# A four-layer graph network: ScalarE clears two accumulators in pieces, and one small gather moves behind 32 others

## The chip, the cores and the metric

The kernel runs on one core of a Trainium2 chip. The metric is device time in microseconds (us): the median of several runs of the whole kernel. The profile is one further execution, recorded by the hardware profiler. Engines are named PE (TensorE's matmuls), PEld (its weight loads), DVE (VectorE), ACT (ScalarE), POOL (GpSimd) and SP (SyncE). A "q" behind a name (DVEq, SPq) is the engine's sequencer: it fetches instructions, loads register values, waits for semaphores and hands work to the engine.

## The reference, cut to what matters

A graph has 6,250 nodes with 128 features and 206,250 edges, sorted by target node. Four graph layers follow one another, each closed by a residual sum and a layer norm. Every layer sums something over the edges of each node:

```python
# layer 1 (eight heads), per edge: message = src * gate * exp(score)
out1 = segment_sum(message, col); norm1 = segment_sum(exp_scores, col)
# layer 2: out = segment_sum(h[src] * exp(clip(leaky(score)))), and its weights' sum
# layer 3: edge_aggr = zeros.at[row].add(edge_features), then a small MLP per node
# layer 4 (last): per node and head keep the eight best edges, softmax, sum h[col]
out4 = segment_sum(alpha[:, :, None] * x_j, row)
x = layernorm(x + elu(out4))
```

The kernel does the sums of layers 2 and 3 in one pass over the edges.

## The kernel before, in words

Nodes stand in 49 blocks of 128 (`NBX` is 50, with a spare block); edges stand in tiles of 128, and four tiles (`G`) make a group. A segment sum runs over "steps": a step k is a group g of edges together with a node block b, so that a group that crosses a block's edge is seen twice. g and b of each step are read at run time from a small table in SBUF (`step_value`, line 358, a TENSOR_LOAD on the sequencer, and `Blocks`, which holds a block number for later use or loads it again when the ring has come round; with the lag of three steps in layer 1, three of every eight steps load twice).

`stage_aggregate` (layer 1, 451 steps). SP loads a group's 256 KB of messages, POOL multiplies them by their weights (line 1006), DVE builds a one-hot matrix of the edges' nodes (line 1043), ACT puts the weights beside the messages (line 1069), PE multiplies the two into PSUM (line 1083), and DVE adds the result to the accumulator `acc` in SBUF, three steps later (line 1056). Rings are eight deep.

`stage_neighbours` (layers 2 and 3, 464 steps; "layer 2" below). SP loads rows of 520 KB a step into a ring of eight, each load once the matmuls and ACT's copy of the step eight earlier are done. POOL makes the score in five small operations (lines 1656 to 1671, each one step behind the one before it), ACT takes the exponential (`weigh`, line 1682) and keeps two columns (`keep`, line 1689), DVE makes the one-hot matrix (line 1704), the weighted rows (line 1711) and, four steps late, the sum into `acc` (line 1723).

In both stages DVE begins with one memset of the whole accumulator, and the first addition waits for it (`s_z`). `pipeline` writes out such a loop: each part is a function with a lag, and the middle is a hardware loop of eight steps.

`stage_last_layer` starts with three loads on SP's queue (`cur`, `prev`, `nxt`), from which DVE makes flags. Then PE, DVE and ACT look up one score for each edge in 416 groups (the counter `s_look`), DVE ranks the scores, and a loop of 464 steps sums the rows. Beside all that POOL gathers a table row for each edge: 1664 indirect DMAs, four to a group, stored to DRAM by SP and loaded again in the sum's loop. Group g's first gather waits until `s_look` has reached 5g/2. Ahead of the first of them POOL waits for the three loads (`s_fl`) and issues one more indirect DMA, `z_start` (line 1861), whose result is wanted after the last lookup.

Of the kernel before, what the change touches and what calls it, by code (L numbers as in the profile page):

```python
# [20 lines left out]
ACT = mybir.ActivationFunctionType  # L21
# [6 lines left out]
P = 128  # L28
C = 128
# [3 lines left out]
NBX = NB + 1  # L33
NP = NB * P
TE = -(-E // P)
G = 4
# [13 lines left out]
KS = GS + NB - 1  # L50
# [928 lines left out]
        back(1)  # L979


def stage_aggregate(nc, v, name, rows, keys, steps, n_steps, groups, weights, heads, acc):


    R = 8
    s_z, s_ld, s_oh = v.sem(name + "_z"), [v.sem(f"{name}_ld{u}") for u in range(R)], v.sem(name + "_oh")
    s_w, s_wc, s_mm, s_add = v.sem(name + "_w"), v.sem(name + "_wc"), v.sem(name + "_mm"), v.sem(name + "_add")
    s_up = v.sem(name + "_up")
    width = C + heads
    with ExitStack() as mem:  # L990
# [7 lines left out]
        with nc.Block() as block:  # L998
# [31 lines left out]

            @block.vector
            def _(dve):
                nc.vector.memset(acc[:, :, 0:width], 0.0).then_inc(s_z, 1)
                nc.vector.tensor_copy(count_up[:, 0:P], v.iota[:, :]).then_inc(s_up, 1)
                dve.wait_ge(s_up, 1)

                blocks = Blocks(nc, dve, steps, groups, 3, R)

                def prepare(k, u, use):
                    g, b = blocks.load(k, u)  # L1040
                    if later(k, R):
                        dve.wait_ge(s_mm, k - R + 1)
                    nc.vector.scalar_tensor_tensor(  # L1043
                        oh[:, u, :, :], count_up[:, None, 0:P].broadcast_to([P, G, P]), v.blk[:, ds(b, 1)],
                        keys[:, ds(g * G, G), None].broadcast_to([P, G, P]), ALU.add,
                        ALU.is_equal).then_inc(s_oh, 1)

                def add(k, u, use):
                    b = blocks.again(k, u)
                    dve.wait_ge(s_mm, k + 1)  # L1050
                    if later(k, 1):
                        dve.wait_ge(s_add, k)
                    else:
                        dve.wait_ge(s_z, 1)
                    here = flat(acc[:, ds(b, 1), 0:width])
                    nc.vector.tensor_tensor(here, here, ps[u % 4][:, 0:width], ALU.add).then_inc(s_add, 1)

                pipeline(dve, n_steps, (prepare, 0), (add, 3), ring=R)

            @block.scalar  # L1060
            def _(act):
                nc.scalar.preload_act_table(ACT.Copy)

                def put(k, u, use):
                    g = step_value(nc, act, steps, 0, k, groups - 1)
                    if later(k, R):
                        act.wait_ge(s_mm, k - R + 1)
                        act.wait_ge(s_z, 1)
                    nc.scalar.activation(wrow[:, u, :, C:width], weights[:, ds(g * G, G), 0:heads],
                                         ACT.Copy).then_inc(s_wc, 1)  # L1070

                pipeline(act, n_steps, (put, 0), ring=R)

            @block.tensor
            def _(pe):
# [545 lines left out]
def stage_neighbours(nc, v, steps, acc, meta, s_meta):  # L1621


    R = 8
    sem = v.sem
# [4 lines left out]
    with ExitStack() as mem:  # L1630
# [5 lines left out]
        with nc.Block() as block:  # L1636
# [39 lines left out]
            @block.scalar  # L1676
            def _(act):
                nc.scalar.preload_act_table(ACT.Exp)

                def weigh(k, u, use):  # L1680
                    act.wait_ge(s_clip, k + 1)
                    nc.scalar.activation(row[:, u, :, C], t[:, u, 4, :], ACT.Exp).then_inc(s_exp, 1)

                def keep(k, u, use):
                    g = step_value(nc, act, steps, 0, k, GS - 1)
                    act.wait_ge(s_at[u], use * 16 + 16)
                    if later(k, 1):
                        act.wait_ge(s_meta, k)
                    nc.scalar.activation(meta[:, ds(g * G, G), :], row[:, u, :, TAKING:RW], ACT.Copy).then_inc(s_meta, 1)

                pipeline(act, KS, (weigh, 0), (keep, 0), ring=R)

            @block.vector
            def _(dve):
                nc.vector.memset(acc[:, :, :], 0.0).then_inc(s_z, 1)

                blocks = Blocks(nc, dve, steps, GS, 4, R)

                def onehot(k, u, use):
# [15 lines left out]
                def add(k, u, use):  # L1715
                    b = blocks.again(k, u)
                    dve.wait_ge(s_mm, k + 1)
                    if later(k, 1):
                        dve.wait_ge(s_add, k)
                    else:  # L1720
                        dve.wait_ge(s_z, 1)
                    here = flat(acc[:, ds(b, 1), :])
                    nc.vector.tensor_tensor(here, here, ps[u % 4][:, 0:ROW], ALU.add).then_inc(s_add, 1)

# [74 lines left out]
def stage_last_layer(nc, v, gathered, steps, acc):  # L1799
# [4 lines left out]
    sem = v.sem  # L1804
# [17 lines left out]
    with ExitStack() as mem:  # L1822
# [34 lines left out]
        with nc.Block() as block:  # L1857
            @block.gpsimd
            def _(pool):
                pool.wait_ge(s_fl, 48)  # L1860
                nc.gpsimd.indirect_dma_start(
                    out=start[:, :], out_offset=None, in_=v.table[:, :],
                    in_offset=bass.IndirectOffsetOnAxis(ap=cur[:, 0:1], axis=0)).then_inc(s_start, 16)
                for t in range(TS):
                    g, j = t // G, t % G
                    u, use = g % U, g // U
                    if j == 0 and g:

# [767 lines left out]
```

## Time and profile before

| | us |
|---|---|
| median of 3 runs (8676.5 to 8685.21) | 8679.93 |
| the profiled execution | 8693.18 |
| its span in the trace | 8691.1 |
| lies around the span | 2.1 |

| engine | busy us | share of the span |
|---|---|---|
| PE | 5916.9 | 68% |
| PEld | 4854.3 | 56% |
| DVE | 6071.0 | 70% |
| ACT | 1746.5 | 20% |
| POOL | 6425.4 | 74% |

No engine is busy all the time: the stages follow one another, and each has its own limit. A share over the whole span therefore says little about a change in one stage; the windows of a stage, the waits in it and the timeline of its start say more. The time of a sequencer's own instructions is not counted as busy time of its engine. "Idle before ... issue" in a timeline means that the engine waited for nothing that the trace shows as a release, only for its next instruction to come.

### The profile page before, as it was taken

The numbers are of one execution on the slowest core, as the hardware profiler recorded it, in microseconds if no ns is written. First come the engines' busy times: TensorE is split into PE (matmuls) and PEld (weight loads), VectorE is DVE, ScalarE is ACT, GpSimd is POOL, SyncE is SP. The second block draws the span as 40 slices with busy tenths as digits, with TensorE's granted clock in tenths as the row PEclk, the third lists the DMA queues.
The fourth block names the chain that finished last, engine by engine and source line by source line (L and its number), as shares of the span: only waits on it lengthen the run. The fifth ranks groups of instructions, "written<-read, shape, count | busy, mean of one in ns | idle before, by whom it ended". The sixth has DMA issues, their size and how long they took to land. (4 is left out here: it accounts for less than half of the span.)

```text
span 8691.1 us, 192168 instructions
## 1 busy us (share of the span) xinstructions
PE 5916.9 (68%) x40472; PEld 4854.3 (56%) x40473; DVE 6071.0 (70%) x12108; ACT 1746.5 (20%) x5063; POOL 6425.4 (74%) x7809
## 2 busy tenths in 40 slices
PE   6666666665788587777777549999588830566442
PEld 4455555553677466666666437777378720455332
DVE  5555555556777887777777448888599899898335
ACT  1111111111211444444444102222500010111000
POOL 6777777776788377777777778887277778877774
PEclk6555555555899799999999669999799965899555
DMA  6778888875477266666666669998189953798664
GB/s 198 218 216 219 219 217 220 218 219 168 130 210 211 70 212 205 207 206 206 207 206 207 211 196 268 273 270 239 35 245 263 260 145 87 197 255 237 163 163 110
DMA packets 1900193, 1739.84 MB, mean 200 GB/s; under 512 B 163065, under 2 KB 1624495, under 8 KB 1899807
## 3 DMA queue, kind: packets, MB, share of 16 engines
q1 hardware_dynamic: 1216980, 816.75, 32.2%
q10 hardware_dynamic: 496812, 471.17, 19.3%
q0 software_dynamic: 186160, 449.72, 18.5%
q14 instruction: 212, 1.74, 0.1%
q8 instruction: 29, 0.48, 0.0%
HBM read 1285.39 MB, written 452.43 MB: 200 GB/s over the span
## 5 line engine op out<-in xcount | busy, mean ns | idle before, releaser
L1877 POOL DMA_INDIRECT z_xg<-table,srci x1664 | 1781.6, 1071 | 512.7 <-issue 457.4
L1414 POOL DMA_INDIRECT sorted<-e_score,srci x1612 | 1628.2, 1010 | 602.8 <-issue 427.2
L461 POOL DMA_INDIRECT g_xg<-table,srci x1612 | 1553.9, 964 | 539.5 <-issue 470.0
L481 PE MATMUL g_psg<-g_wg,g_eT 128*128 128x136 f32 x3224 | 1027.5, 474 | 0.0
L1957 PE MATMUL z_ps<-z_wrow,z_oh 128*128 128x132 f32 x3712 | 652.1, 330 | 501.9 <-issue 332.6
L1735 PE MATMUL n_ps<-n_row,n_oh 128*128 128x257 f32 x3712 | 881.2, 389 | 93.2 <-DVE n_row L1711 79.3
L1957 PEld LDWEIGHTS z_ps<-z_wrow,z_oh 128*128 128x128 f32 x3712 | 559.4, 228 | 594.6 <-issue 557.3
L481 PEld LDWEIGHTS g_psg<-g_wg,g_eT 128*128 128x128 f32 x3224 | 769.3, 324 | 191.9 <-issue 191.9
L1735 PEld LDWEIGHTS n_ps<-n_row,n_oh 128*128 128x128 f32 x3712 | 677.7, 190 | 298.0 <-issue 216.4
L479 PE MATMUL g_psg<-g_bias,g_ones 3*128 3x272 bf16 x806 | 318.4, 395 | 675.6 <-DVE g_es L570 646.8
L1473 PE MATMUL m_psx<-acc,e_score 128*128 x3608 | 600.5, 317 | 197.8 <-DVE e_score L1598 122.9
L568 DVE TENSOR_TENSOR g_y<-g_psg,g_xg 128x512 f32<-128x512 f32 x403 | 278.5, 691 | 604.7 <-DMA g_xg<-table,srci 590.0
L1473 PEld LDWEIGHTS m_psx<-acc,e_score 128*128 128x128 f32 x3608 | 507.9, 217 | 259.3 <-issue 258.3
L1913 PE MATMUL z_ps<-z_tab,z_ohlo 128*128 128x200 bf16 x4992 | 599.6, 249 | 74.4 <-DVE z_e L2059 69.7
L1598 DVE SCALAR_TENSOR_TENSOR e_score<-e_score,follows,m_psx 128x516 f32 x451 | 339.4, 753 | 370.6 <-ACT e_score L1524 312.2
L522 ACT ACTIVATE g_psg<-g_psg 128x512 f32<-128x512 f32 x403 | 234.5, 582 | 1807.6 <-PE g_psg L481 1807.6
L1083 PE MATMUL ag_ps<-ag_wrow,ag_oh 128*128 128x136 f32 x3608 | 488.9, 289 | 101.2 <-DVE ag_oh L1043 101.1
L2138 DVE TENSOR_TENSOR z_wrow<-z_buf,z_e 128x512 f32<-128x512 f32 x464 | 317.6, 684 | 334.9 <-DMA z_buf<-gathered 334.7
L1463 PE MATMUL m_psl<-m_cnt,e_score 128*128 128x100 f32 x3224 | 550.4, 299 | 0.2 <-DVE e_score L1573 0.2
L1006 POOL TENSOR_TENSOR ag_wrow<-ag_buf,e_score 128x512 f32<-128x512 f32 x451 | 467.6, 1060 | 99.7 <-PE ag_ps L1083 88.5
L479 PEld LDWEIGHTS g_psg<-g_bias,g_ones 3*128 3x128 bf16 x806 | 79.3, 98 | 800.0 <-issue 764.9
L1083 PEld LDWEIGHTS ag_ps<-ag_wrow,ag_oh 128*128 128x128 f32 x3608 | 444.4, 190 | 145.8 <-issue 114.3
(426 smaller groups left out, 12696.0 us busy)
## 6 DMA issues: line engine op xcount, KB each, us to landing
n_row<-sorted SPq DMA_DIRECT2D x464, 520.0 KB, 4.4
z_buf<-gathered ACTq DMA_DIRECT2D x464, 256.0 KB
g_keys<-dst_row ACTq DMA_DIRECT2D x451, 256.0 KB, 3.8
ag_buf<-gated SPq DMA_DIRECT2D x451, 256.0 KB, 3.3
m_keys<-dst_row ACTq DMA_DIRECT2D x451, 256.0 KB
gathered<-z_xg SPq DMA_DIRECT2D x416, 256.0 KB
gated<-g_y SPq DMA_DIRECT2D x403, 256.0 KB
g_eT<-in_attr_t SPq DMA_DIRECT2D x402, 256.0 KB
```

Source lines behind the costliest of these rows:

```text
L461: nc.gpsimd.indirect_dma_start(out=xg[:, u, j, :], out_offset=None, in_=v.table[:, :], in_offset=bass.IndirectOffsetOnAxis(ap=v.srci[:, t: ...
L479: nc.tensor.matmul(psg[u % 2][:, h, 0:H * W], ones[:, :], bias[:, :], start=True, stop=False)
L481: last = nc.tensor.matmul(psg[u % 2][:, h, j * W:(j + 1) * W], eT[:, u % R, (h * H + j) * P:(h * H + j + 1) * P], wg[:, :], start=False, s ...
L1006: engine.tensor_tensor(wrow[:, u, :, 0:C].rearrange("p t (h c) -> p t h c", h=heads), buf[:, u, :, :].rearrange("p t (h c) -> p t h c", h= ...
L1083: last = nc.tensor.matmul(ps[u % 4][:, 0:width], oh[:, u, j, :], wrow[:, u, j, 0:width], start=(j == 0), stop=(j == G - 1))
L1414: nc.gpsimd.indirect_dma_start(out=v.sorted[:, :], out_offset=bass.IndirectOffsetOnAxis(ap=place[:, t:t + 1], axis=0), in_=rows[:, u, j, : ...
L1463: nc.tensor.matmul(to, oht[:, u, j * P:(j + 1) * P], before, start=True, stop=False)
L1473: last = nc.tensor.matmul(psx[u % 2][:, j // 2, (j % 2) * WH:(j % 2 + 1) * WH], hot_t[:, u, j * P:(j + 1) * P], flat(held[:, ds(b, 1), :]) ...
L1735: last = nc.tensor.matmul(ps[u % 4][:, 0:ROW], oh[:, u, j, :], row[:, u, j, 0:ROW], start=(j == 0), stop=(j == G - 1))
L1877: nc.gpsimd.indirect_dma_start(out=xg[:, u, j, :], out_offset=None, in_=v.table[:, :], in_offset=bass.IndirectOffsetOnAxis(ap=v.dsti[:, t: ...
L1913: nc.tensor.matmul(to, ohlo[:, u, edges], tab[:, n, :, :], start=(n == 0), stop=False)
L1957: last = nc.tensor.matmul(bank[u % 4 // 2][:, u % 2, 0:width], oh[:, u, j, :], wrow[:, u, j, 0:width], start=(j == 0), stop=(j == G - 1))
```

## The change

In the two stages the memset on DVE goes. ACT writes the zeros instead, as four copies of a constant zero, each over a quarter of the accumulator's blocks (12, 13, 12 and 13). In layer 1 a piece follows each of ACT's first four steps. In layer 2 the first piece comes ahead of the loop, and the other three follow the first three steps. The addition of a step waits for as many pieces as its block can lie in (1 to 4), and this wait stands in every addition, also in the hardware loop, where it is for 4; before, only the first addition waited for `s_z`. ACT's own wait for `s_z` in layer 1 goes. In the last layer, the wait for the three loads and the `z_start` gather move from POOL's start to the front of group 8, behind 32 gathers.

```diff
+def zero_pieces(nc, v, acc, width, sem):
+
+
+    def zero(n, u, use):
+        a, z = (NBX * n // 4, NBX * (n + 1) // 4)
+        nc.scalar.activation(acc[:, a:z, 0:width], v.zeros[:, None, 0:1].broadcast_to([P, z - a, width]),
+                             ACT.Copy).then_inc(sem, 1)
+
+    return zero
+
+
+def zeroed(k):
+
+    return 4 if not isinstance(k, int) else min(4, sum(k >= NBX * n // 4 for n in range(4)))
...
 def stage_aggregate(nc, v, name, rows, keys, steps, n_steps, groups, weights, heads, acc):
-                nc.vector.memset(acc[:, :, 0:width], 0.0).then_inc(s_z, 1)
...
                     if later(k, 1):
                         dve.wait_ge(s_add, k)
-                    else:
-                        dve.wait_ge(s_z, 1)
+                    dve.wait_ge(s_z, zeroed(k))
...
                     if later(k, R):
                         act.wait_ge(s_mm, k - R + 1)
-                        act.wait_ge(s_z, 1)
...
-                pipeline(act, n_steps, (put, 0), ring=R)
+                pipeline(act, n_steps, (put, 0), (zero_pieces(nc, v, acc, width, s_z), 0, 4), ring=R)
...
 (stage_neighbours)
-                pipeline(act, KS, (weigh, 0), (keep, 0), ring=R)
+                zero = zero_pieces(nc, v, acc, 2 * C + 1, s_z)
+                zero(0, 0, 0)
+                pipeline(act, KS, (weigh, 0), (keep, 0), (lambda n, u, use: zero(n + 1, u, use), 0, 3), ring=R)
...
-                nc.vector.memset(acc[:, :, :], 0.0).then_inc(s_z, 1)
...
                     if later(k, 1):
                         dve.wait_ge(s_add, k)
-                    else:
-                        dve.wait_ge(s_z, 1)
+                    dve.wait_ge(s_z, zeroed(k))
...
 (stage_last_layer)
-                pool.wait_ge(s_fl, 48)
-                nc.gpsimd.indirect_dma_start(
-                    out=start[:, :], out_offset=None, in_=v.table[:, :],
-                    in_offset=bass.IndirectOffsetOnAxis(ap=cur[:, 0:1], axis=0)).then_inc(s_start, 16)
                 for t in range(TS):
                     g, j = t // G, t % G
+                    if t == 8 * G:
+                        pool.wait_ge(s_fl, 48)
+                        nc.gpsimd.indirect_dma_start(
+                            out=start[:, :], out_offset=None, in_=v.table[:, :],
+                            in_offset=bass.IndirectOffsetOnAxis(ap=cur[:, 0:1], axis=0)).then_inc(s_start, 16)
```

## Rows read from the trace of the kernel before

**Rows 1.** Windows of two stretches: from:to us, then the columns of the first line.
```profile
core 0: us, PE busy (x) PEld busy (x) DVE busy (x) ACT busy (x) POOL busy (x), PEclk, DMA share, GB/s
2247.00:2860.00 613.00, 507.65 (x3761) 462.42 (x3760) 453.04 (x913) 116.91 (x465) 492.24 (x474) 0.97 0.67 197
5145.00:6065.00 920.00, 881.22 (x3712) 677.66 (x3712) 781.99 (x1391) 193.77 (x928) 767.43 (x2318) 1.00 0.91 264
```

**Rows 2.** Timeline, layer 1's start: start us, us, engine, line, operation, [idle before, releaser].
```profile
2289.45 5.72 DVE L1033 MEMSET acc<- 128x6800 f32 x1 [33.13 <-issue]
2291.66 1.06 POOL L1006 TENSOR_TENSOR ag_wrow<-ag_buf,e_score 128x512 f32<-128x512 f32 x1 [9.64 <-DMA ag_buf<-gated]
2295.86 2.76 DVE L1043 SCALAR_TENSOR_TENSOR ag_oh<-ag_up,blk,keys 128x512 f32<-128x512 f32 x4 [0.49 <-DVE ag_up L1034]
2296.67 12.85 PE L1083 MATMUL ag_ps<-ag_wrow,ag_oh 128*128 128x136 f32 x88 [29.48 <-DVE ag_oh L1043]
```

**Rows 3.** Timeline of VectorE (DVE) in layer 1's loop, one-hot instructions.
```profile
2330.11 0.75 DVE L1043 SCALAR_TENSOR_TENSOR ag_oh<-ag_up,blk,keys 128x512 f32<-128x512 f32 x1 [0.54 <-issue]
...
2331.11 0.75 DVE L1043 SCALAR_TENSOR_TENSOR ag_oh<-ag_up,blk,keys 128x512 f32<-128x512 f32 x1
...
2332.10 0.75 DVE L1043 SCALAR_TENSOR_TENSOR ag_oh<-ag_up,blk,keys 128x512 f32<-128x512 f32 x1
```

**Rows 4.** VectorE's sequencer (DVEq) by line, layer 1: count, ns min/median/max, first and last start.
```profile
L358 DVEq TENSOR_LOAD <-steps_e x632: 296/302/326, 2295.4 to 2857.1; - x158
L358 DVEq FUSED_REGOPS  x540: 57/57/64, 2315.5 to 2850.7; - x180
...
L1052 DVEq EVENT_SEMAPHORE  x396: 21/21/21, 2300.0 to 2857.4; - x198
L1052 DVEq ALU_OP  x54: 40/40/40, 2316.0 to 2843.4; - x54
...
L1056 DVEq FUSED_REGOPS  x451: 57/57/71, 2298.9 to 2857.5; - x151
...
L1043 DVEq FUSED_REGOPS  x469: 46/186/199, 2295.8 to 2855.2; - x157
L1043 DVEq ALU_OP  x432: 40/40/40, 2315.4 to 2851.4; - x144
```

**Rows 5.** The same for a loop of stage_move whose instructions wait for three semaphores.
```profile
L1594 DVEq EVENT_SEMAPHORE  x1: 21/21/21, 3001.7 to 3001.7; - x1
...
L1596 DVEq EVENT_SEMAPHORE  x450: 49/262/5072, 3005.5 to 5080.3; - x150
```

**Rows 6.** Timeline, layer 2's start.
```profile
5132.99 10.77 DVE L1695 MEMSET acc<- 128x12850 f32 x1 [41.60 <-issue]
...
5137.44 6.92 POOL L1656 TENSOR_TENSOR n_t<-n_row 128x4 f32<-128x4 f32 x1 [2.94 <-DMA n_row<-sorted]
...
5146.93 0.21 ACT L1682 ACTIVATE n_row<-n_t 128x4 f32<-128x4 f32 x1 [15.40 <-POOL n_t L1671]
```

**Rows 7.** Windows, layer 2's start.
```profile
5145.00:5148.00 3.00, 0.00 (x0) 0.02 (x1) 0.83 (x2) 0.42 (x2) 3.00 (x15) 0.50 0.04 13
```

**Rows 8.** Waits in layer 2: engine, line, releaser: us in total, times, longest.
```profile
DVE n_oh L1704 <- issue: 38.0, 131, 0.4
```

**Rows 9.** ScalarE's longest plain fp32 pass (last layer's update), by line.
```profile
L1163 ACT ACTIVATE up_T<-up_T x1: 5538/5538/5538, 8621.6 to 8621.6; 128x6400 f32<-128x6400 f32 x1
```

**Rows 10.** Timeline of GpSimd (POOL) at the last layer's start.
```profile
6298.85 2.53 POOL L1861 DMA_INDIRECT z_start<-table,z_cur  x1 [17.99 <-DMA z_nxt<-sorted_row]
...
6319.27 0.94 POOL L1877 DMA_INDIRECT z_xg<-table,srci  x1 [5.94 <-PE z_ps L1914]
```

**Rows 11.** The last layer's 1664 gathers by line, and waits ahead of them.
```profile
L1877 POOL DMA_INDIRECT z_xg<-table,srci x1664: 939/946/14414, 6301.7 to 8594.7; - x185
...
  issue: 457.4, 1501
...
  PE z_ps L1914: 12.9, 24
```

## The prediction

> **What bounds the kernel now.** I read the windows by stage first, then the timeline at each place the diff touches, then the sequencers' rows by line, and last the waits.
>
> In layer 1 no engine fills its window: PE is busy 507.65 of 613.00 us, POOL 492.24, DVE 453.04 [rows 1]. The timeline says what is missing. In DVE's loop a one-hot starts 0.99 us after the one before it, or, in other steps, only after 0.54 us of idle time put down to issue [rows 3]. The sequencer explains both. It makes 632 register loads of 302 ns in 451 steps, that is 451 and 181 second ones, about three in eight steps [rows 4]; the steps with a second load are the slow ones. A short step has one load (302), one FUSED_REGOPS at L358 (57), one at L1056 (57), one at L1043 (186), one ALU_OP (40) and one EVENT_SEMAPHORE (21): 663 ns [rows 4]. The step is 990 ns [rows 3], so 327 ns for six instructions, 54 ns each, pass between them. The EVENT_SEMAPHORE at L1052 is 21 ns at minimum, median and maximum in all 396 cases [rows 4]: it never waits for PE. The reader is to see that **the DVE sequencer, not an engine, sets layer 1's pace**, so that each instruction put into this loop is paid in full.
>
> In layer 2 DMA moves 264 GB/s, with PE busy 881 and DVE 782 of 920 us [rows 1], 1.98 us for each of 464 steps. DVE's idle time for issue is 38.0 us in 131 steps [rows 8]: there the sequencer is late in little more than a quarter of the steps.
>
> In the last layer POOL's gathers run from 6301.7 to 8594.7 [rows 11], and nearly all their idle time is the 0.3 us between two of them (457.4 us, 1501 times). Only one wait is real: the fifth gather waits 5.94 us for the lookups [rows 10]. **POOL's stream sets this layer's end.**
>
> **The change part by part.** The sum is made against the profiled execution (8693.18 us: span 8691.1 and 2.1 around it), which is 13.3 us above the median of 8679.93; the difference is carried over to the median.
>
> *Layer 1, the start.* The memset (5.72 us) goes, and the one-hots can begin near 2290 in place of 2295.86 [rows 2]. What is late next is POOL: its first product ends at 2291.66 + 1.06 = 2292.72. PE can start then in place of 2296.67: **-3.9 us**. ACT pays for the zeros. A long fp32 pass there takes 5538 ns for 6400 elements, 0.87 ns each [rows 9]; a piece has 1632 or 1768, so 1.4 to 1.5 us and some 0.2 to start. Four pieces with ACT's own small copies are done about 8 us after the first copy; PE's fourth step can't come before 2292.7 + 3 x 1.2, when ACT's fourth copy is done. Nothing. If PE had to wait for ACT in each of the four, the start would gain 1 us less or so.
>
> *Layer 1, the loop.* The new wait is one constant comparison in each addition. The trace has no such addition with three waits here, but it has the pattern elsewhere. Where an instruction waits for two semaphores, one EVENT_SEMAPHORE of 21 ns stands ahead of it, the other wait riding on an instruction that is there anyway [rows 4]. Where it waits for three, the row is still one EVENT_SEMAPHORE for each of the 450 steps, of 49 ns at least; the first step, with two waits, has 21 [rows 5]. So the third wait costs 28 ns in seven of eight steps. In the eighth, 54 times, there is no EVENT_SEMAPHORE now, since an ALU_OP at L1052 carries a wait [rows 4]; with three waits one has to be added: 21 + 54 = 75 ns. Sum: 397 x 0.028 + 54 x 0.075 = 11.1 + 4.1 = **+15.2 us**. Bounds: 0, if the wait rides on an instruction that is there; 451 x 0.075 = +33.8 if each gets an instruction of its own. I take the middle, as row 5 is this very pattern on this very engine. ACT's removed wait gives nothing, since ACT waits for PE.
>
> The Trainium skill, "Advanced Engine Details and Errata" (Network/Comms), gives 50 to 100 ns for the sequencer to read a semaphore. By that the 451 waits would cost an estimated 23 to 45 us; rows 4 and 5 show less for an added wait, so it stands beside the first rival below and not in the sum.
>
> *Layer 2, the start.* The memset of 10.77 us ends at 5143.76, and a POOL operation on 128x4 elements, 6.92 us long, lies under it to 5144.36; the first exponential follows at 5146.93 [rows 6]. From 5145 to 5148 the DMA queues are all but idle (0.04): the eight slots are full and the first isn't free [rows 7]. Without the memset the first exponential may come some 5 us earlier. But three of ACT's pieces, 3084 to 3341 elements, 2.9 us each by the same price, stand between its first four steps, each some 1 us over the pace of 1.98: 3 us are lost again, and only then do the earlier loads count. I take **-4 us**; bounds -7 (the whole idle stretch is filled) and +3 (POOL is no earlier and ACT's pieces delay three steps).
>
> The Trainium skill, "SBUF — State Buffer", says that a DVE instruction with at most one SBUF input outside the two-port modes doesn't contend with GpSimd. The 6.92 us of rows 6 speak against it, the 1.06 us of POOL under layer 1's memset in rows 2 for it. By the rule POOL is no earlier, and the upper bound of this term would hold.
>
> *Layer 2, the loop.* The same wait, 464 times. It can be felt where DVE stood idle for issue: 131 x 0.028 = 3.7 us, half of it hidden since DMA, POOL and PE share the limit: **+2 us**. Bounds: 0, and 407 x 0.028 + 57 x 0.075 = +16 if all are felt.
>
> *Last layer.* Before the fifth gather POOL has time to spare; there `z_start` is free now, and its removal gives nothing. Among the 32nd and 33rd it is not: 0.94 + 0.30 us of a stream that never waits, **+1.2 us**. Its wait for the three loads is long over by then, and its row is wanted only after the last lookup. The first four gathers can now issue some 10 us earlier, while the three loads are in flight (POOL stands idle for 17.99 us until they land [rows 10]). Four gathers of 128 x 136 fp32 are 0.28 MB; at the 0.26 MB per us of rows 1 they can hold the last load back by 1.1 us, and with it flags, lookups and the fifth gather. I take **+0.8**, bounds 0 and 1.1.
>
> **Sum:** -3.9 + 15.2 - 4 + 2 + 1.2 + 0.8 = **+11.3 us**, 8704.5 for a profiled execution and **8691 us** for the median, 0.13% up. A measurement of this kernel can tell about 0.2%, that is 17.4 us, from no change.
>
> **The rivals.**
> 1. *Each added wait is an instruction of its own* (75 ns). For it: the eighth steps. Against it: rows 5. Layer 1's loop costs 33.8 in place of 15.2: the sum is +29.9, 8710 us, slower. It decides from about 47 ns per wait: there layer 1's loop costs 21.3 and the sum passes 17.4.
> 2. *The wait is free*: it rides on the FUSED_REGOPS that computes the address of `acc`. For it: the compiler already lets waits ride. Against it: that instruction is there now, and an EVENT_SEMAPHORE stands ahead of it all the same. Only the starts and the last layer are left: -3.9 - 4 + 2 = -5.9, 8674 us, no change that can be told.
> 3. *Layer 2 pays in full*: the sequencer is late there more often than 131 steps show, and POOL gains nothing at the start. +3 and +16 in place of -4 and +2: the sum is +32, or +23 with one half of each, 8703 us, slower. Against it: the sequencer has no load to repeat in five of eight steps, and 264 GB/s of DMA is near another limit.
> 4. *The starts give much more than their idle time*, because a ring that fills earlier runs steadier: faster by 20 us, 8660. Nothing in the rows speaks for it.
>
> **How the numbers follow.** My case 0.60, its own range 8682 to 8700, with an eighth of it past 17.4 us; rival 1 0.17; rival 2 0.12; rival 3 0.07; rival 4 0.04. Slower by over 0.2%: 0.08 + 0.17 + 0.05 = 0.30; faster by over 0.2%: 0.04 and a little of rival 2, 0.05; within 0.2%: 0.65. The range leaves out rival 4 and the far ends of 1 and 3: 8673 to 8713.
>
> **What would show it.** Layer 1's DVEq row of the new wait's line: EVENT_SEMAPHORE in all 450 steps at 49 or 50 ns (my case), twice as many rows of 21 ns (rival 1), or none added (rival 2). PE's first matmul of layer 1 some 3.9 us sooner after ACT's table load, and the stage from there to its end some 15 us longer. Layer 2's first exponential some 5 us sooner after its table load, the next three about 3 us apart, the DMA queues not idle. The fifth gather no earlier than now, the last one later by 1 to 2 us. The prediction is wrong if layer 1's loop isn't bound by the sequencer in the steps where I say so: then PE or POOL swallows the 28 ns, and the gain at the starts is what is left.

## The result, and the profile after

The changed kernel takes **8695.15 us** (median of 20 runs, 8684.74 to 8707.39); the kernel before, run beside it, 8682.02 (20 runs, 8669.02 to 8695.0). The ratio is **1.0015** with a 95% interval of 1.0009 to 1.0022, that is +13.1 us, with +8 to +19 in the interval. The forecast was +11.3 and 8691: slower, by less than 0.2%.

The profiled execution took 8695.34 us, with a span of 8693.6. That is only 2.5 us above the span before (8691.1), and the reader should not take it for the effect: the first instruction of layer 1 (ACT's table load) comes at 2287.97 before and at 2282.91 after, although nothing is changed ahead of it. A single profile has several microseconds of such scatter outside the changed stages, so everything below is measured from a mark inside the stage.

Layer 1's start after, a timeline (the columns are those of rows 2). L987 is the line of the clearing pieces:

```profile
2282.91 1.28 ACT L1076 ACT_TABLE_LOAD   x1 [19.80 <-PEq L650]
...
2283.74 2.76 DVE L1058 SCALAR_TENSOR_TENSOR ag_oh<-ag_up,blk,keys 128x512 f32<-128x512 f32 x4 [0.50 <-DVE ag_up L1049]
...
2284.34 1.54 ACT L987 ACTIVATE acc<-zeros 128x1632 f32<-128x1632 f32 x1
...
2286.50 1.06 POOL L1022 TENSOR_TENSOR ag_wrow<-ag_buf,e_score 128x512 f32<-128x512 f32 x1 [9.55 <-DMA ag_buf<-gated]
...
2287.66 12.64 PE L1096 MATMUL ag_ps<-ag_wrow,ag_oh 128*128 128x136 f32 x81 [25.55 <-POOL ag_wrow L1022]
...
2289.16 1.66 ACT L987 ACTIVATE acc<-zeros 128x1768 f32<-128x1768 f32 x1
2289.97 0.30 DVE L1070 TENSOR_TENSOR acc<-acc,ag_ps 128x136 f32 x1 [3.47 <-PE ag_ps L1096]
```

PE's first matmul waited for DVE's one-hot before [rows 2]; now its releaser is POOL's product, which is what the prediction named as late next. The one-hots follow DVE's small copy at once. The matmul comes 3.45 us after ACT's first copy (2284.20 to 2287.66), where it was 7.40 us before (2289.26 to 2296.67 [rows 2]): 3.95 us sooner.

Layer 1's loop after, by line on VectorE, sequencer and engine: count, ns min/median/max, first and last start. The first row is the line of the new wait.

```profile
L1068 DVEq EVENT_SEMAPHORE  x451: 21/50/50, 2286.1 to 2863.7; - x151
...
L1070 DVEq FUSED_REGOPS  x451: 57/57/71, 2289.9 to 2863.8; - x151
L1070 DVE TENSOR_TENSOR acc<-acc,ag_ps x451: 282/285/298, 2290.0 to 2863.9; 128x136 f32 x151
```

Where 396 events of 21 ns stood [rows 4], 451 stand now, and their median is 50. Counted one by one, 396 of them take 49 or 50 ns and 55 take 21: the first step, and the 54 eighth ones, in which an event has been added. From the first to the last address computation of the additions (FUSED_REGOPS) it is 573.9 us (2289.9 to 2863.8) in place of 558.6 (2298.9 to 2857.5 [rows 4]): 15.3 us longer. The short steps, in a timeline of VectorE:

```profile
2559.31 0.75 DVE L1058 SCALAR_TENSOR_TENSOR ag_oh<-ag_up,blk,keys 128x512 f32<-128x512 f32 x1
2559.98 0.28 DVE L1070 TENSOR_TENSOR acc<-acc,ag_ps 128x136 f32 x1
2560.33 0.75 DVE L1058 SCALAR_TENSOR_TENSOR ag_oh<-ag_up,blk,keys 128x512 f32<-128x512 f32 x1
2561.00 0.29 DVE L1070 TENSOR_TENSOR acc<-acc,ag_ps 128x136 f32 x1
2561.34 0.75 DVE L1058 SCALAR_TENSOR_TENSOR ag_oh<-ag_up,blk,keys 128x512 f32<-128x512 f32 x1
```

A one-hot starts 1.02 and 1.01 us after the one before it, against 1.00 and 0.99 in rows 3. From the additions' starts in the middle 400 steps, a turn of eight takes 10.218 us after and 9.951 before: 0.267 us more, where the terms of the prediction make 7 x 0.028 + 0.075 = 0.271.

Layer 2's start after, a timeline:

```profile
5134.06 1.28 ACT L1691 ACT_TABLE_LOAD   x1 [45.83 <-PEq L2506]
...
5135.35 2.77 ACT L987 ACTIVATE acc<-zeros 128x3084 f32<-128x3084 f32 x1
...
5138.13 0.75 DVE L1717 SCALAR_TENSOR_TENSOR n_oh<-iota,blk,n_row 128x512 f32<-128x512 f32 x1 [42.90 <-DMA n_row<-sorted]
5140.70 0.21 POOL L1669 TENSOR_TENSOR n_t<-n_row 128x4 f32<-128x4 f32 x1 [2.43 <-DMA n_row<-sorted]
...
5144.69 0.21 ACT L1695 ACTIVATE n_row<-n_t 128x4 f32<-128x4 f32 x1 [6.57 <-POOL n_t L1684]
...
5145.25 2.97 ACT L987 ACTIVATE acc<-zeros 128x3341 f32<-128x3341 f32 x1
...
5148.13 0.19 ACT L1695 ACTIVATE n_row<-n_t 128x4 f32<-128x4 f32 x1
...
5150.98 0.19 ACT L1695 ACTIVATE n_row<-n_t 128x4 f32<-128x4 f32 x1
...
5154.06 0.19 ACT L1695 ACTIVATE n_row<-n_t 128x4 f32<-128x4 f32 x1
```

POOL's second operation takes 0.21 us in place of 6.92 [rows 6]. The first exponential comes 10.63 us after ACT's table load (5134.06 to 5144.69), before it was 16.68 (5130.25 to 5146.93 [rows 6]): 6.05 us sooner. DVE's first one-hot comes 4.07 us after the table load; before, it came at the memset's end, 13.43 us after:

```profile
5143.68 1.28 DVE L1704 SCALAR_TENSOR_TENSOR n_oh<-iota,blk,n_row 128x512 f32<-128x512 f32 x2
```

ACT's pieces then space the exponentials 3.44, 2.85 and 3.08 us apart; before, they came 1.9 us apart, so at the fourth one 3.7 of the 6.05 us are given back. They don't stay lost: the next two exponentials follow within 0.6 us, and the tenth one comes 32.10 us after the table load, before 36.08, a lead of 4.0 us.

The DMA queues show what the earlier start is worth. Both kernels first fill the eight free slots, at some 355 GB/s. Then the queues stand idle until a slot comes free: 7.5 us before, 1.5 us after. Windows of these idle stretches (columns as in rows 1), first before, then after, with the end of the filling ahead of each:

```profile
5138.25:5143.25 5.00, 0.00 (x0) 0.00 (x0) 5.00 (x1) 0.00 (x0) 5.00 (x1) 0.50 1.10 356
5145.00:5152.50 7.50, 4.49 (x11) 3.59 (x12) 4.07 (x6) 1.25 (x6) 7.50 (x26) 0.50 0.01 5
...
5143.80:5147.50 3.70, 1.73 (x4) 1.48 (x5) 1.35 (x2) 2.57 (x3) 3.14 (x14) 0.50 1.09 355
5149.00:5150.50 1.50, 1.50 (x7) 1.17 (x6) 0.71 (x2) 1.50 (x1) 1.50 (x7) 0.69 0.02 8
```

The last layer, a timeline of POOL: the fifth large gather, and the small one in its new place:

```profile
6312.18 0.94 POOL L1890 DMA_INDIRECT z_xg<-table,srci  x1 [26.60 <-PE z_ps L1927]
...
6347.07 0.94 POOL L1890 DMA_INDIRECT z_xg<-table,srci  x1 [0.30 <-issue]
6348.32 0.94 POOL L1876 DMA_INDIRECT z_start<-table,z_cur  x1 [0.30 <-issue]
6349.57 1.06 POOL L1890 DMA_INDIRECT z_xg<-table,srci  x1 [0.30 <-PE z_ps L1927]
```

All large gathers by line, the first and last start behind the durations:

```profile
L1890 POOL DMA_INDIRECT z_xg<-table,srci x1664: 940/944/14412, 6280.7 to 8596.9; - x185
```

The first gather starts at 6280.7, 0.6 us after the first of the three loads is issued (6280.06); before, it was 14 us (6287.73 to 6301.7 [rows 11]). The fifth gains nothing from it: it starts 32.12 us after that issue (6312.18), against 31.54 before (6319.27 [rows 10]). `z_start` sits in a stream without slack, 1.25 us of it.

### The profile page after: what moved, and what is told of

It reads as the page before. It is cut to its first block and busy times, and to the rows that moved or that the text cites. A ratio compares the mean times of both kernels' runs of the same rounds, so it can differ in the third digit from the quotient of the medians.

```text
span 8693.6 us, 191841 instructions
## 1 busy us (share of the span) xinstructions
PE 5937.6 (68%) x40472; PEld 4881.8 (56%) x40473; DVE 6053.8 (70%) x12106; ACT 1761.5 (20%) x5071; POOL 6413.4 (74%) x7809
## 3 DMA queue, kind: packets, MB, share of 16 engines
q1 hardware_dynamic: 1216980, 816.75, 31.9%
## 5 line engine op out<-in xcount | busy, mean ns | idle before, releaser
L1476 PE MATMUL m_psl<-m_cnt,e_score 128*128 128x100 f32 x3224 | 559.0, 302 | 0.1
L1476 PEld LDWEIGHTS m_psl<-m_cnt,e_score 128*128 128x128 f32 x3224 | 526.2, 205 | 2.2 <-issue 0.3
```

What stands on the lines that cost most here:

```text
L1476: nc.tensor.matmul(to, oht[:, u, j * P:(j + 1) * P], before, start=True, stop=False)
```

## The experiments

Each kernel was timed against the kernel before in the same session, or has a single profiled run (numbers 1, 8 and 9), whose time alone says little. The table puts the stages of all profiles side by side. Its numbers are differences of two instructions' starts in one trace: (a) layer 1, ACT's first copy to PE's first matmul; (b) layer 1, first to last addition; (c) layer 2, last gather of the stage ahead to the first exponential; (d) the same gather to layer 2's last addition; (e) last layer, issue of `z_cur`'s load to the last addition.

| kernel | a | b | c | d | e |
|---|---|---|---|---|---|
| before | 7.40 | 558.6 | 24.5 | 941.3 | 2320.9 |
| before, again | 7.41 | 558.8 | 24.5 | 940.5 | 2323.5 |
| layer 1: the wait alone | 7.41 | 573.2 | 24.5 | 938.4 | 2319.3 |
| layer 1: two waits | 7.41 | 612.5 | 24.6 | 944.5 | 2311.3 |
| layer 1: pieces, no wait in the loop | 3.64 | 559.2 | 24.5 | 940.7 | 2322.3 |
| layer 2 as changed | 7.41 | 558.3 | 18.5 | 937.3 | 2317.2 |
| layer 2: pieces, no wait in the loop | 7.40 | 558.5 | 18.6 | 933.9 | 2316.9 |
| layer 2: memset in ten | 7.41 | 558.7 | 19.0 | 935.5 | 2311.9 |
| layer 2: one-hots behind the memset | 7.40 | 558.6 | 18.7 | 941.1 | 2322.3 |
| the small gather alone | 7.41 | 558.6 | 24.5 | 941.3 | 2322.8 |
| changed | 3.45 | 573.9 | 18.4 | 929.6 | 2331.0 |
| changed, again | 3.52 | 573.7 | 18.1 | 940.4 | 2326.2 |
| changed, no waits in the loops, early gather | 3.76 | 559.0 | 18.1 | 934.0 | 2324.2 |
| the same, layer 2's pieces ahead | 3.47 | 559.4 | 20.6 | 934.9 | 2320.6 |

Columns a, b and c hardly scatter between kernels that share the edit (by 0.3, 0.7 and 0.5 us at most). Columns d and e scatter by 6 and 12 us where the stage's code is that of before, and that sets what can be said of them. Column d can be divided at the 40th addition of layer 2. From the last gather ahead to that addition it takes 109.5 to 111.4 us in the six profiles with layer 2 as before (mean 110.6), 104.9 to 105.3 in the three with the pieces and the wait, 104.2 to 106.0 in the three with the pieces and no wait in the loop, 106.0 in number 8 and 108.5 in number 9. Nearly all the scatter of column d lies behind that addition.

**1. The kernel before, once more.** No edit: how far does one profile lie from another?

> The kernel before, unchanged, profiled once more: it gives the size of what one stage's length differs by between two executions. If layer 2's loop (20th to 440th addition, 827.5 us in the first profile) and the last layer (from its first load to its last addition, 2320.9 us) come back within 2 us, the 6 us by which layer 2's loop was shorter and the 10 us by which the last layer was longer after the change are the change's; if they differ by 5 to 10 us, they are the spread of single executions. Layer 1's loop (20th to 440th addition, 523.45 us) should come back within 0.3 us on the theory that a sequencer paces it, since nothing there waits for memory.

Measured: 8692.48 us in one run, span 8690.5. Every column but the last agrees within 0.9 us with the first profile. The last layer differs by 2.6 us, layer 2 by 0.9. What follows: layer 1's length is a quantity that can be read to a microsecond. Two profiles are too few for the scatter of the others; the whole table shows more.

**2. Layer 1: the wait alone.** The memset on DVE stays, and the comparison stands in each addition:

```diff
-                    else:
-                        dve.wait_ge(s_z, 1)
+                    dve.wait_ge(s_z, 1)
```

> The kernel before with one edit: in layer 1 every addition also waits for the memset's semaphore, which has long been set. Theory (the DVE sequencer paces the loop and pays 28 ns for a third wait, 75 ns where none had an instruction of its own): layer 1's loop is 15 us longer, its start and all else as before, 8697 us, ratio 1.0017. Rival (the 15 us of the changed kernel come from ACT's pieces or from chance): no change, 1.000.

Measured: 1.0019, interval 1.0010 to 1.0028 (medians 8719.90 and 8706.62). VectorE by line in layer 1:

```profile
L1053 DVEq EVENT_SEMAPHORE  x451: 21/50/50, 2295.9 to 2869.7; - x151
...
L1055 DVE TENSOR_TENSOR acc<-acc,ag_ps x451: 282/286/298, 2296.7 to 2869.9; 128x136 f32 x151
```

The row of the event is the one of the changed kernel, to the nanosecond, and the loop is 573.2 us long: +14.6 over before. Its wait is for a count reached before the first matmul, so nothing is waited for; reading it is the whole cost. What follows: the wait alone makes the slowdown of layer 1.

**3. Layer 1: the pieces without the wait in the loop.** The pieces are done within ten steps, so only the steps written out ahead of the hardware loop need to look:

```diff
-                    else:
-                        dve.wait_ge(s_z, 1)
+                    if isinstance(k, int) and k < 16:
+                        dve.wait_ge(s_z, 4 if k >= 8 else zeroed(k))
```

> Layer 1's accumulator is cleared by ACT in four pieces as in the changed kernel, but only the additions ahead of the hardware loop wait for them (the ninth for all four); layers 2 and last are those before. Theory: the start gains 3.9 us, the loop is as before (523.5 us from the 20th to the 440th addition), so 8678 us, ratio 0.9996. Rival (the pieces on ACT themselves lengthen the loop): 8692 us, 1.001 or more.

Measured: 0.9999, interval 0.9990 to 1.0008. The start is 3.8 us shorter (column a), the loop 0.4 to 0.6 longer (b), and the hardware loop has its events of 21 ns again. Twelve steps written out ahead of it have events of 49 or 50 ns, which is most of these 0.4 to 0.6 us. What follows: start and loop are two separate terms, and the first can be had without the second. The timed ratio alone could not have told -3.3 us from nothing.

**4. Layer 1: two added waits.** Number 2 with a second comparison:

```diff
+                    dve.wait_ge(s_z, 1)
+                    dve.wait_ge(s_up, 1)
```

> The kernel before with two constant waits more in every addition of layer 1, four in all. Theory: the third wait shares the EVENT_SEMAPHORE of the second (28 ns more), the fourth needs another instruction (75 ns more): 0.103 x 451 = 46 us in layer 1's loop, 8728 us, ratio 1.0054. Rival (28 ns for each wait whatever their number): 25 us, 1.0029. Second rival (75 ns each): 68 us, 1.0078.

Measured: 1.0066, interval 1.0051 to 1.0081; layer 1's loop 612.5 us, +53.9. VectorE's events by line:

```profile
L1053 DVEq EVENT_SEMAPHORE  x396: 21/21/21, 2299.9 to 2911.1; - x198
L1054 DVEq EVENT_SEMAPHORE  x451: 49/50/50, 2298.1 to 2911.2; - x151
```

The third wait of an instruction lengthened an event that was there, from 21 to 50 ns; the fourth needs one of its own. And the waits ahead of DVE and POOL, engine, line, releaser: us in total, times, longest:

```profile
POOL ag_wrow L1006 <- PE ag_ps L1083: 125.1, 219, 0.8
...
DVE ag_oh L1043 <- issue: 126.4, 230, 0.7
```

DVE stands idle for its sequencer 230 times, where it is 94.1 us in 176 in the changed kernel, and POOL waits for PE, which waits for DVE. The second wait cost 39.3 us (612.5 - 573.2). Of these 1.6 us are the 55 events that grow from 21 to 50 ns only now; the rest is 95 ns for each of the 396 further events, more than the 75 ns forecast for an event and its gap, and the 53.9 us are 8 more than the 46 expected. By the additions' starts in the middle 400 steps, five of a turn's eight steps are 0.067 to 0.071 us longer than in the changed kernel, about the forecast price; one is no longer, and two are longer by 0.17 and 0.19. What those two wait for is not settled. What follows: a price near rival 1's exists, one wait further on.

**5. Layer 2 as changed, the rest as before.**

```diff
+                zero(0, 0, 0)
+                pipeline(act, KS, (weigh, 0), (keep, 0), (lambda n, u, use: zero(n + 1, u, use), 0, 3), ring=R)
...
-                nc.vector.memset(acc[:, :, :], 0.0).then_inc(s_z, 1)
...
+                    dve.wait_ge(s_z, zeroed(k))
```

> Layer 2 alone as in the changed kernel (ACT clears in pieces, every addition waits for them); layer 1 and the last layer are those before. The profiles of the kernels before and of three others so far have layer 2 at 938.4 to 944.5 us from the last gather of the stage ahead of it to its last addition, the changed kernel 929.6. Theory (the first exponential comes 6 us sooner, and the loop's rest is little changed): 930 to 936 us for that stretch, 8674 us on the scale of the first median, ratio 0.9993. Rival from the prediction (the added wait is felt in the loop): 945 us or more, ratio 1.001.

Measured: 0.9996, interval 0.9987 to 1.0005. The first exponential is 6.0 us sooner (c), layer 2 ends 4.0 us sooner (d), at 937.3 us: just above the 930 to 936 that were expected, well below the rival's 945.

**6. Layer 2: pieces, no wait in the loop.** Number 5, and in its addition:

```diff
-                    dve.wait_ge(s_z, zeroed(k))
+                    if isinstance(k, int) and k < 16:
+                        dve.wait_ge(s_z, 4 if k >= 8 else zeroed(k))
```

> As the run before, but only the additions ahead of layer 2's hardware loop wait for the pieces. Theory (the wait is mostly hidden in this layer): the stretch is 0 to 2 us shorter than with the wait. Rival (each of the 464 waits is paid, 28 or 75 ns): 10 to 16 us shorter.

Measured: 0.9993, interval 0.9984 to 1.0002; column d 933.9. The two differ by 3.4 us in one profile each and by 0.0003 in time, both inside the scatter. Over all profiles with the pieces, the three with the wait in layer 2's loop have a mean of 935.8 us in column d and the three without it 933.9 to 934.9, mean 934.2. What follows: the wait costs 1.5 us in layer 2 by these means, and a term of +2 is neither confirmed nor refuted; the 16 us of rival 3 would show, and don't.

DVE's idle time for issue, which the prediction used for this term [rows 8], can't tell: 38.0 us in 131 steps before, 34.6 in 114 in the changed kernel. In layer 1, where the same wait made the loop 15.3 us longer, that row hardly moved either. The rows of layer 1, before and changed, and of layer 2, changed:

```profile
DVE ag_oh L1043 <- issue: 93.4, 176, 0.6
DVE ag_oh L1058 <- issue: 94.1, 176, 0.6
...
DVE n_oh L1717 <- issue: 34.6, 114, 0.5
```

All 451 steps of layer 1 paid, not the 176 that this view counts as idle for issue.

**7. The small gather alone.** The last layer's edit, nothing else.

```diff
-                pool.wait_ge(s_fl, 48)
-                nc.gpsimd.indirect_dma_start(
...
+                    if t == 8 * G:
+                        pool.wait_ge(s_fl, 48)
+                        nc.gpsimd.indirect_dma_start(
```

> The small gather of the last layer behind eight groups, all else as before. Theory: three loads land about 1.1 us later, the fifth gather starts 0.6 us later counted from the first load, and one gather of 1.25 us more stands in POOL's stream: 1 to 2 us, which a single execution can't show beside the spread of this layer's lookups and gathers (2311 to 2324 us so far); ratio 1.0002. Rival (the last layer's extra 10 us in the changed kernel's profile come from the move): ratio 1.001, the layer at 2330 us again.

Measured: 1.0005, interval 0.9996 to 1.0014. DVE's flags, which need the three loads, start 11.8 us after the first load's issue, against 10.9 before; the stretch from the 5th to the 101st gather takes 124.5 us, against 122.7. The whole layer takes 2322.8 us, inside the scatter of unchanged code and below the rival's 2330. The timed interval holds both the expected 1.0002 and the rival's 1.001.

**8. Layer 2: the memset in ten pieces on DVE.** Does a memset hold POOL, as the prediction read rows 6? Each piece is 1.13 us:

```diff
-                nc.vector.memset(acc[:, :, :], 0.0).then_inc(s_z, 1)
+                for n in range(10):
+                    last = nc.vector.memset(acc[:, 5 * n:5 * n + 5, :], 0.0)
+                last.then_inc(s_z, 1)
```

> The kernel before with layer 2's memset on DVE cut into ten of 1285 elements, 1.1 us each. Theory (the memset holds POOL's operations back while it runs, as a DVE one-hot with two SBUF inputs does): POOL's second operation no longer lasts 6.9 us but ends with the slice it meets, and the first exponential comes 1 to 3 us sooner after ACT's table load (16.7 us before). Rival (what holds POOL is the one-hot behind the memset, or a load that hasn't landed): the second operation still ends only after the last slice, and the first exponential stays at 16.7 us.

Measured: 8682.06 us in one run. Timeline:

```profile
5138.78 1.13 DVE L1696 MEMSET acc<- 128x1285 f32 x1 [0.22 <-issue]
5140.13 1.13 DVE L1696 MEMSET acc<- 128x1285 f32 x1 [0.22 <-issue]
5140.26 0.21 POOL L1656 TENSOR_TENSOR n_t<-n_row 128x4 f32<-128x4 f32 x1 [2.92 <-DMA n_row<-sorted]
5140.43 0.26 POOL L1660 TENSOR_SCALAR n_t<-n_t 128x4 f32<-128x4 f32 x1
...
5145.32 1.92 POOL L1667 TENSOR_TENSOR n_t<-n_t 128x4 f32<-128x4 f32 x1
5145.51 1.13 DVE L1696 MEMSET acc<- 128x1285 f32 x1 [0.22 <-issue]
5146.56 1.29 DVE L1706 SCALAR_TENSOR_TENSOR n_oh<-iota,blk,n_row 128x512 f32<-128x512 f32 x2
```

POOL's operation runs in 0.21 us in the middle of a memset. So a memset doesn't hold POOL. Neither the theory (1 to 3 us sooner) nor the rival (no change) came true: the first exponential is 5.5 us sooner with the zeros still on DVE. Only at the last piece, behind which the first one-hot stands, is a POOL operation long (1.92 us). At the 40th addition layer 2 is 4.6 us ahead of the mean before, where the kernels with ACT's pieces are 5.5 ahead. So most of the gain of layer 2's start can be had without ACT, as far as one profile shows.

**9. Layer 2: the whole memset, the one-hots kept out of DVE's queue.** What held POOL then? Behind the whole memset the next DVE instruction is a one-hot, which reads two tensors from SBUF. Here it isn't handed to the engine before the memset is over:

```diff
                 nc.vector.memset(acc[:, :, :], 0.0).then_inc(s_z, 1)
+                dve.wait_ge(s_z, 1)
```

> The kernel before with one wait more: after layer 2's whole memset, DVE waits for it to end before it hands its first one-hot to the engine. Theory (what holds POOL's operation for 6.9 us is the one-hot, which reads two operands in SBUF and stands in the engine's queue behind the memset, since with the sliced memset POOL ran freely): POOL's second operation lasts 0.2 us under the whole memset, and the first exponential comes 5 us sooner after ACT's table load (11.5 us in place of 16.7), though DVE does the same work in the same order. Rival (a long memset holds POOL by itself): 6.9 and 16.7 us as before.

Measured: 8694.45 us in one run. Timeline:

```profile
5132.33 10.77 DVE L1695 MEMSET acc<- 128x12850 f32 x1 [41.58 <-issue]
...
5136.49 0.21 POOL L1656 TENSOR_TENSOR n_t<-n_row 128x4 f32<-128x4 f32 x1 [2.79 <-DMA n_row<-sorted]
...
5140.47 0.21 ACT L1682 ACTIVATE n_row<-n_t 128x4 f32<-128x4 f32 x1 [9.60 <-POOL n_t L1671]
...
5143.61 1.41 DVE L1705 SCALAR_TENSOR_TENSOR n_oh<-iota,blk,n_row 128x512 f32<-128x512 f32 x2 [0.51 <-DVE acc L1695]
```

The memset is the same 10.77 us, and POOL's 6.92 us of rows 6 are 0.21 us under it. The first exponential comes 10.9 us after the table load (11.5 expected), where the six profiles with the old order have 16.67 or 16.68. So it was the one-hot waiting in the queue. Rows 2 fit this: behind layer 1's memset stands a copy with one input, and POOL's product under it takes its usual 1.06 us. What an earlier start of POOL and ACT alone buys is less clear. DVE's first one-hot still comes at the memset's end, 5143.61 here, and in number 8 too. The 40th addition is 2.1 us ahead of the mean before in this profile and 4.6 in number 8; the whole layer takes 941.1 us here (d), as before, and 935.5 there. The cause of that difference stays open.

**10. The changed kernel without the waits in the loops, the small gather behind the first group.** `z_start` goes where POOL waits for the lookups anyway, and both loops get the edit of number 6:

```diff
-                    if t == 8 * G:
+                    if t == G:
```

> The changed kernel with two edits: in both layers only the additions ahead of the hardware loop wait for the pieces, and the small gather of the last layer stands behind the first group's four gathers, in the time in which POOL waits for the lookups anyway. Theory: 3.8 us less in layer 1, 5 to 7 us less in layer 2, nothing in the last layer: ratio to the kernel before 0.9989, 8672 us on the scale of the first median. Rival (a gain at the start of layer 2 is lost again before its end): 0.9995 or above.

Measured: 0.9995, interval 0.9986 to 1.0004. That is the rival's value; the expected 0.9989 is just inside the interval. Layer 2 takes 934.0 us (d), 7 below the mean before, so its gain isn't lost before its end. Timeline of POOL:

```profile
6292.39 2.48 POOL L1878 DMA_INDIRECT z_start<-table,z_cur  x1 [6.57 <-DMA z_nxt<-sorted_row]
6313.28 0.95 POOL L1892 DMA_INDIRECT z_xg<-table,srci  x1 [18.41 <-PE z_ps L1929]
```

The gather stands between two waits of 6.57 and 18.41 us, and the stretch from the 5th to the 101st large gather is back at 122.5 us.

**11. The same, with layer 2's four pieces ahead of its loop.**

```diff
                 zero = zero_pieces(nc, v, acc, 2 * C + 1, s_z)
-                zero(0, 0, 0)
+                for n in range(4):
+                    zero(n, 0, 0)
```

> As the run before, but in layer 2 all four of ACT's pieces come ahead of the loop. Theory (pieces between the exponentials cost about 1 us a step): the first exponential comes 2 us later than with the pieces spread (some 13 us after ACT's table load begins, in place of 10.6), the fourth 3 us sooner (17 in place of 20), layer 2 another 1 to 3 us shorter, ratio 0.9987. Rival (DMA and the ring make up for either order): the same as the run before within 1 us.

Measured: 0.9992, interval 0.9983 to 1.0001. ACT writes for 11.5 us before its first exponential, which is 2 us later than in number 10, but the fourth is 2.4 us sooner: 17.26 against 19.64 us after the table load. But layer 2 as a whole is no shorter (934.9 against 934.0, d), as the rival had it and not the theory. The ratio is the lowest of all, 0.0024 below the changed kernel's in the same session; it is not clear of the kernel before, nor of numbers 5, 6 and 10 (0.9996, 0.9993 and 0.9995).

**12. The changed kernel, once more.**

> The changed kernel once more, in the same session as the two better versions. Layer 1's loop (20th to 440th addition) within 0.5 us of its first 537.47 us. Layer 2 from the last gather ahead of it to its last addition: 929.6 us again if its 11.5 us gain is the change's own, 935 to 937 if it was partly the spread, as in the runs with layer 2's parts alone. The last layer: 2331 us again if the change makes it 10 us longer, 2312 to 2325 if that was the spread. Ratio 1.0015.

Measured: 1.0016, interval 1.0007 to 1.0026. Layer 1 repeats to 0.2 us. Layer 2 doesn't: 940.4 in place of 929.6, and above the 935 to 937 that a part of scatter should have given. The last layer takes 2326.2 us, 1 above the 2312 to 2325 expected of scatter and 5 below the first profile.

## Why the prediction was right

**Layer 1's start, -3.9: measured -3.95.** POOL's product is late next, at the place and the time that rows 2 give, and ACT's pieces took 1.54 and 1.66 us where 1.6 to 1.7 was worked out. That they cost nothing held (number 3: -3.8, and the loop within 0.6).

**Layer 1's loop, +15.2: measured +15.3**, and +14.6 with the wait alone. Each part was seen: 396 events longer by 29 ns, 54 new ones of 21 ns, a turn of eight 0.267 us longer. The argument that decided it was that the sequencer sets the pace. It was drawn from adding up its instructions to the step's length [rows 3, 4], and number 2 is its proof: an event that waits for nothing, 29 ns longer in 396 steps and new in 54, lengthened the stage by what it takes. Rival 2 (free) fell with it, and rival 1 (75 ns each) with the events' durations.

**Layer 2's start, -4: measured -5.5. Loop, +2: not resolved.** The start is the stretch to the 40th addition. It is 5.5 us shorter in the three profiles with the pieces and the wait (104.9 to 105.3 us against 109.5 to 111.4), and as much without the wait in the loop. The forecast was too small by 1.5 us: the prediction lost 3 us for good to ACT's pieces, but after the fourth exponential, where 3.7 us are given back, most of the lead returns. Behind the 40th addition the three profiles with the wait take 824.7 to 835.3 us, mean 830.6, and the six with layer 2 as before 828.9 to 833.1, mean 830.5. A term of +2 can't be told from nothing there. It was also drawn from a row that doesn't measure it, as number 6 shows. Together the two terms were -2 and measured about -5: the six profiles with the memset whole in its old place and order have a mean of 941.1 us in column d, the three with the wait and the pieces 935.8. The -11.7 us between the first two profiles is mostly scatter, as number 12 shows. Rival 3 (layer 2 pays in full) fell: the layer became shorter. Rival 4 (the starts give 20 us or more) fell too: with both starts and no wait in the loops the ratio is 0.9995 (number 10).

**A step read wrongly, with a right outcome.** The prediction took the 6.92 us of rows 6 as speaking against the rule of the Trainium skill, "SBUF — State Buffer", section "Who interferes with whom", by which a DVE instruction with at most one SBUF input, outside the two-port modes, doesn't contend with GpSimd. Numbers 8 and 9 agree with the rule: the memset doesn't hold POOL (0.21 us beneath it). What did is the two-input one-hot behind it. POOL was freed all the same, because with the memset gone the one-hot no longer waited in the queue; that was luck. Where the pieces stayed on DVE, the same reading did give a wrong forecast: number 8 expected 1 to 3 us and measured 5.5.

**Last layer, +1.2 and +0.8.** The place of `z_start` cost what was said: the stretch from the 5th to the 101st gather takes 124.2 to 124.9 us in the three profiles that have it there and 122.0 to 123.3 in the eleven that don't, 1.9 us more on average; a little more than its own 1.25. The loads are later by 1.0 us (flags at 11.8 to 12.0 against 10.8 to 11.1 us after the issue), and the fifth gather by 0.5 us on average (31.9 to 32.9 us after the issue in the three, 31.3 to 32.8 in the nine with `z_start` in its old place), so that the forecast 0.8 is neither confirmed nor refuted. Together +2.4.

**The sum.** -3.95 + 15.3 - 5.3 + 2.4 = +8.4 us out of localized terms, at the lower edge of the measured +8 to +19. So the total came closer to the forecast +11.3 than its parts did: layer 2 gave more than forecast, and some 5 us that no term has were added. The ratios of the single edits add up to 0.0019 - 0.0001 - 0.0004 + 0.0005 = 0.0019 (numbers 2, 3, 5, 7) beside 0.0015 and 0.0016, but each of the four is known to 0.0009 only. Column e shows where the missing 5 us may lie: 2331.0, 2326.2 and 2322.8 with the small gather behind eight groups, 2311.3 to 2323.5 in the nine profiles with it at the start. It isn't in the waits. From the fifth gather on, the 1660 gathers' own durations sum to 1778.8 us in the changed kernel's profile and to 1770.8 before, and between profiles of unchanged code they go from 1759.8 to 1772.6. Whether the move lengthens the gathers or the three profiles fell high stays open.

## What to carry to other kernels

Before a wait is put into a loop, add up the sequencer's rows of that loop: where loads, register operations and gaps make up the step, a wait that is never waited for still costs its time in every step (here 29 ns for a longer event, 65 to 95 for a further one), and a one-time condition belongs into the steps written out ahead of the loop. The idle time for issue in the waits view doesn't show this: it stood still in layer 1 while the loop grew by 15 us. An early start is worth what the next-late engine lets through, so read its row before counting the stall as gain. And compare stages from marks inside them: layer 1's loop could be read to 0.5 us in a kernel whose runs differ by 26.

## What the runs showed of the hardware that had not been expected

- A DVE instruction with two SBUF inputs that waits in the queue behind a 10.77 us memset held POOL's 128x4 operation for 6.92 us [rows 6]; with the same memset and the one-hot held back it took 0.21 us. By the trace the block comes from an instruction that hasn't begun, not from the one that runs.
- In this loop DVE's second wait was an event of 21 ns, the third made the same event 50 ns, and the fourth was a further event of 21 ns, which cost 95 ns on average.
- ACT writes fp32 zeros at DVE's pace: 1632, 1768, 3084 and 3341 elements per partition took 1.54, 1.66, 2.77 and 2.97 us, some 0.84 ns for each further element and 0.2 us to start. DVE's memsets of 6800 and 12850 elements took 5.72 and 10.77 us, 0.83 ns for each further one.
